# Cross-attention on one core: the first two blocks of x in halves of 256 columns, on ScalarE's queue

## What is computed

```
memory_proj = einsum('bme,de->bmd', memory, W_mem)
scores = einsum('bnd,bmd->bnm', x, memory_proj) / sqrt(512)
attn = softmax(scores)
memory_context = einsum('bnm,bmd->bnd', attn, memory_proj)
gate = sigmoid(einsum('bnf,df->bnd', concat([x, memory_context]), W_gate) + b_gate)
fused = x + gate * memory_context
out = fused * rsqrt(mean(fused**2) + 1e-6) * norm_w
```

## Time and profile before

| | us |
|---|---|
| median of 3 runs | 124.92 |
| lowest, highest | 123.68, 125.67 |
| the profiled execution, whole | 122.92 |
| its span in the trace | 121.2 |
| PE busy | 112.8 (93%) |
| DVE busy | 76.1 (63%) |
| ACT busy | 55.1 (45%) |
| POOL busy | 19.0 (16%) |

### The profile page before, as it was taken

One profiled execution on the slowest core, in us unless ns is written; L12 is line 12 of the kernel. 1 busy time (PEld: TensorE's weight loads), 2 busy tenths in 40 slices (PEclk: granted clock), 3 DMA queues, 4 the chain that ended last, 5 costly groups with the idle time before them and its releaser, 6 DMA issues.

```text
span 121.2 us, 1531 instructions
## 1 busy us (share of the span) xinstructions
PE 112.8 (93%) x529; PEld 92.8 (77%) x529; DVE 76.1 (63%) x115; ACT 55.1 (45%) x99; POOL 19.0 (16%) x25
## 2 busy tenths in 40 slices
PE   6899999999999999999999999999899999999900
PEld 6778788688888888888888888888588888888800
DVE  0398979977999700459982899947620032764791
ACT  4587575468967930942305365252500030423231
POOL 2000000000000499691000301010200000011040
PEclk9999999999999999999999999999999999999995
DMA  3999993236864690000455583847720000053204
GB/s 69 316 378 323 390 355 96 103 139 176 233 225 175 197 286 16 0 0 0 173 157 195 177 288 131 275 170 209 224 87 0 5 0 0 0 171 89 87 18 155
DMA packets 11095, 18.45 MB, mean 152 GB/s; under 512 B 1232, under 2 KB 4048, under 8 KB 11088
## 3 DMA queue, kind: packets, MB, share of 16 engines
q1 hardware_dynamic: 10656, 17.70, 43.9%
q10 hardware_dynamic: 432, 0.66, 1.9%
HBM read 14.16 MB, written 4.19 MB: 151 GB/s over the span
## 4 chain that ended last, share of the span: by engine, by line
PE 57%; DVE 14%; DMA 13%; issue 7%; ACT 3%; SPq 2%; POOL 1%; POOLq 1%; DVEq 0%; ACTq 0%
PE acc L758 18%; PE wide L708 12%; PE acc L683 8%; DMA ring<-passage 5%; DMA passage<-ring 5%; PE wide L736 5%; PE wide L786 4%; PE wide L774 4%; DVE neg_max L479 4%; PE wide L801 3%; DMA ring<-xT 3%; PE wide L722 3%; DVE ring L497 3%; DVE pT_lo L503 2%; SPq L277 2%
## 5 line engine op out<-in xcount | busy, mean ns | idle before, releaser
L322 POOL TENSOR_TENSOR rstd<-mean_sq,neg_half 128x1 f32<-128x1 f32 x8 | 5.4, 672 | 57.6 <-ACT squares L393 56.5
L520 DVE TENSOR_TENSOR wgT_lo<-acc,wgT_hi 128x512 fp32r<-128x512 f32 x4 | 2.6, 686 | 17.6 <-ACT wgT_hi L382 17.6
L708 PE MATMUL wide<-ctxT_hi,qT_lo 128*128 128x512 f32 x32 | 12.6, 393 | 0.0
L708 PE MATMUL wide<-ctxT_hi,qT_hi 128*128 128x512 f32 x32 | 12.6, 392 | 0.0
L357 ACT ACTIVATE probs<-wide,neg_max 128x1024 f32<-128x1024 f32 x8 | 8.9, 1115 | 8.0 <-DVE neg_max L479 8.0
L708 PE MATMUL wide<-ctxT_lo,qT_hi 128*128 128x512 f32 x32 | 12.5, 390 | 0.0
L386 ACT ACTIVATE gate<-gate 128x512 f32<-128x512 f32 x8 | 5.1, 632 | 15.1 <-DVE gate L530 15.1
L317 POOL TENSOR_TENSOR wgT_lo<-ring,wgT_hi 128x512 fp32r<-128x512 f32 x4 | 5.4, 1374 | 39.7 <-ACT wgT_hi L343 39.7
L479 DVE TENSOR_REDUCE neg_max<-wide 128x1 f32<-128x1024 f32 x8 | 9.8, 1222 | 2.2 <-PE wide L708 1.9
L758 PE MATMUL acc<-pT_lo,ctxN_hi 128*128 128x512 f32 x32 | 10.0, 393 | 0.5 <-DVE pT_lo L503 0.5
L758 PE MATMUL acc<-pT_hi,ctxN_lo 128*128 128x512 f32 x32 | 9.9, 390 | 0.0
(11 more groups left out here) (89 smaller groups left out, 244.8 us busy)
## 6 DMA issues: line engine op xcount, KB each, us to landing
ring<-ctxT SPq DMA_DIRECT2D x8, 256.0 KB, 4.1
ring<-w_gateT SPq DMA_DIRECT2D x8, 256.0 KB, 4.9
ring<-ctxN SPq DMA_DIRECT2D x8, 256.0 KB, 4.3
xr<-x_rows SPq DMA_DIRECT2D x8, 256.0 KB, 3.2
passage<-ring SPq DMA_DIRECT2D x4, 512.0 KB, 2.9
ring<-passage SPq DMA_DIRECT2D x16, 128.0 KB, 2.8
out<-res SPq DMA_DIRECT2D x7, 256.0 KB, 2.0
ring<-xT SPq DMA_DIRECT2D x6, 256.0 KB, 5.6
```

What stands on the lines that cost most here:

```text
L322: nc.gpsimd.tensor_tensor(rstd[:, col], mean_sq[:, col], neg_half[:], ALU.pow)\
L708: last = nc.tensor.matmul(wide[:, banks("scores", j), h], qT_s[left][:, c, rows], ctxT_s[right][:, c, cols], start=(c == 0 and (left, righ ...
```

## The change

The first two x blocks of batch 0 become four: x0 columns 0 to 255, x0 columns 256 to 511, x1 likewise. Each has its own place in the block list, its own ring slot (only half used) and its own splits. All four are issued by ACT. The block list has 40 entries instead of 38, so the hand-written numbers and `FIRST_ON_POOL` rise by two. On PE the 12 matmuls of 512 columns for k = 0 and 1 become 24 of 256.

```
-        def xT_block(b, k):
-            block(("xT", b, k), xT[b, :, k], xT_s, b, k)
+        def xT_block(b, k, cols=slice(0, N)):
+            block(("xT", b, k, cols.start), xT[b, :, k, cols], xT_s, b, k, cols)
...
+        X_HALVES = (slice(0, N // 2), slice(N // 2, N))
         wm_block(0, 0)
-        xT_block(0, 0)
+        for cols in X_HALVES:
+            xT_block(0, 0, cols)
         wm_block(1, 0)
-        xT_block(0, 1)
+        for cols in X_HALVES:
+            xT_block(0, 1, cols)
...
-        FIRST_ON_POOL = 28
-
-        BY_ACT = (index_of["xT", 0, 0], index_of["xT", 0, 1])
+        FIRST_ON_POOL = 30
+
+        BY_ACT = [index_of["xT", 0, k, cols.start] for k in range(2) for cols in X_HALVES]
...
-            split_hi(0, 1, 2, 3, 4, 5, 6, 7, 8)
+            split_hi(0, 1, 2, 3, 4, 5, 6, 7, 8, 9, 10)
...
-            split_lo(0, 1, 2, 3, 4, 5, 6, 7, 8)
+            split_lo(0, 1, 2, 3, 4, 5, 6, 7, 8, 9, 10)
...
-                    wm_i, xT_i = index_of["wm", c, 2 * k // KD], index_of["xT", b, k]
-                    for left, right in ((HI, HI), (LO, HI), (HI, LO)):
-                        if (left, right) == (HI, HI):
-                            wait_hi(pe, wm_i)
-                            wait_hi(pe, xT_i)
...
-                        last = nc.tensor.matmul(acc[:, c], wm_s[left][:, c, k], xT_s[right][:, b, k],
-                                                start=(k == 0 and (left, right) == (HI, HI)),
...
+                    wm_i = index_of["wm", c, 2 * k // KD]
+                    for cols in X_HALVES if b == 0 and k < 2 else (slice(0, N),):
+                        xT_i = index_of["xT", b, k, cols.start]
+                        for left, right in ((HI, HI), (LO, HI), (HI, LO)):
...
+                            last = nc.tensor.matmul(acc[:, c, cols], wm_s[left][:, c, k], xT_s[right][:, b, k, cols],
+                                                    start=(k == cols.start == 0 and (left, right) == (HI, HI)),
```

More of the change, by code:

```diff
@@ L394, in mean_square @@
                                      accum_out=mean_sq[:, j:j + 1]).then_inc(squared, 1)
-            split_hi(0, 1, 2, 3, 4, 5, 6, 7, 8)
+            split_hi(0, 1, 2, 3, 4, 5, 6, 7, 8, 9, 10)
             query_hi(0, 0)
-            split_hi(9, 10)
+            split_hi(11, 12)
             query_hi(0, 1)
-            split_hi(11, 12, 13)
+            split_hi(13, 14, 15)
             exponentials(0)
-            split_hi(14, 15)
+            split_hi(16, 17)
             exponentials(1)
-            split_hi(16)
+            split_hi(18)
             exponentials(2)
             turned_hi(0)
-            split_hi(17, 18)
+            split_hi(19, 20)
             turned_hi(1)
@@ L410, in _ @@
             query_hi(1, 0)
-            split_hi(19)
+            split_hi(21)
             query_hi(1, 1)
             turned_hi(2)
-            split_hi(20, 21)
+            split_hi(22, 23)
             weight_hi(0)
             turned_hi(3)
-            split_hi(22, 23)
+            split_hi(24, 25)
             weight_hi(1)
-            split_hi(*range(24, 34))
+            split_hi(*range(26, 36))
             attended_hi(0, 0)
             attended_hi(0, 1)
-            split_hi(*range(34, NB))
+            split_hi(*range(36, NB))
             exponentials(4)
@@ L582, in finish_last @@
                                         ALU.mult).then_inc(last_left, 1)
-            split_lo(0, 1, 2, 3, 4, 5, 6, 7, 8)
+            split_lo(0, 1, 2, 3, 4, 5, 6, 7, 8, 9, 10)
             query_lo(0, 0)
-            split_lo(9, 10)
+            split_lo(11, 12)
             query_lo(0, 1)
-            split_lo(11, 12)
+            split_lo(13, 14)
             row_max(0)
-            split_lo(13)
+            split_lo(15)
             row_max(1)
             normalize(0)
-            split_lo(14)
+            split_lo(16)
             row_max(2)
             normalize(1)
-            split_lo(15)
+            split_lo(17)
             normalize(2)
-            split_lo(16)
+            split_lo(18)
             turned_lo(0)
-            split_lo(17)
+            split_lo(19)
             row_max(3)
             turned_lo(1)
-            split_lo(18)
+            split_lo(20)
             normalize(3)
             query_lo(1, 0)
-            split_lo(19)
+            split_lo(21)
             query_lo(1, 1)
             turned_lo(2)
-            split_lo(20)
+            split_lo(22)
             weight_lo(0)
-            split_lo(21)
+            split_lo(23)
             turned_lo(3)
-            split_lo(22, 23)
+            split_lo(24, 25)
             weight_lo(1)
-            split_lo(24, 25, 26, 27)
+            split_lo(26, 27, 28, 29)
             attended_lo(0, 0)
@@ L673, in queries @@
                 for k in ks:
-                    wm_i, xT_i = index_of["wm", c, 2 * k // KD], index_of["xT", b, k]
-                    for left, right in ((HI, HI), (LO, HI), (HI, LO)):
-                        if (left, right) == (HI, HI):
-                            wait_hi(pe, wm_i)
-                            wait_hi(pe, xT_i)
[L679 to L682, removed]
-                        last = nc.tensor.matmul(acc[:, c], wm_s[left][:, c, k], xT_s[right][:, b, k],
-                                                start=(k == 0 and (left, right) == (HI, HI)),
-                                                stop=(k == KD - 1 and (left, right) == (HI, LO)))
+                    wm_i = index_of["wm", c, 2 * k // KD]
+                    for cols in X_HALVES if b == 0 and k < 2 else (slice(0, N),):
+                        xT_i = index_of["xT", b, k, cols.start]
+                        for left, right in ((HI, HI), (LO, HI), (HI, LO)):
+                            if (left, right) == (HI, HI):
+                                wait_hi(pe, wm_i)
+                                wait_hi(pe, xT_i)
+                            elif left == LO:
+                                wait_lo(pe, wm_i)
+                            else:
+                                wait_lo(pe, xT_i)
+                            last = nc.tensor.matmul(acc[:, c, cols], wm_s[left][:, c, k], xT_s[right][:, b, k, cols],
+                                                    start=(k == cols.start == 0 and (left, right) == (HI, HI)),
+                                                    stop=(k == KD - 1 and (left, right) == (HI, LO)))
                 if ks[-1] == KD - 1:
```

## The result

The changed kernel takes 128.1 us in the median of six executions (127.55 to 130.55), the kernel before 125.3 (six, 123.08 to 126.0): slower, by a ratio of 1.0346 with a 95% interval of 1.0231 to 1.0462. The profiled execution took 128.24 us, its span is 126.5. One thing has to be said for the ratio to be understood: three of the six executions of the kernel before (125.67 to 126.0 us) are left out of the comparison as disturbed, as are 18 of its 60 in all jobs together (125.06 to 128.44), so the ratio is that of 127.96 to 123.68 us, where the two medians above stand at 1.022.

A forecast was written before the change was run, and what follows sets the result against it. PE, busy for 93% of the span, was taken to bound the kernel; the first stage's terms summed to +0.3 us, passed on unchanged, taking the median from 124.92 to 125.2 us, range 123.9 to 126.5.

The forecast's parts named there:

- (c): PE's queries: 24 matmuls of 256 columns at 0.125 us replace 12 of 512, +0.27 us, covered by gaps.
- (a): ScalarE's queue: four issues instead of two delay the table load to 2.60; ACT's first split +0.1 us, at about 4.08.
- (b): First x half lands at about 4.0 instead of 4.56, so PE begins at about 4.95, 0.4 us earlier.
- The cover: PE's first gaps, 0.4 us together, plus 0.4 from (b), were to hide the narrow matmuls' +0.27 us.
- (d): DMA: x rows of 1 KB instead of 2 KB add 0.2 us; fourth x block lands at 8.28 instead of 8.08.
- (e): Arrival order: fourth half lands at 6.6 to 7.3, last x split at 8.4 to 8.5; PE's matmul +0.3 us.
- (f): Ring: two more slots delay the first two ctxT loads to about 4.9 and 5.4; priced at nothing.
- Rival 2: DMA: 1 KB rows as dear as 2 KB ones, fourth x block 1.36 us later; 126.3 us, chance 0.15.
- Rival 3: PE's clock falls to 1.2 GHz at the start, costing about 3 to 5 us; 128 to 130, chance 0.02.

The follow-up runs named there:

- TensorE's part alone: The kernel before with only the 12 products of k = 0 and 1 as 24 of 256 columns, loads and splits whole: 127.32 us, ratio 1.0244.
- the 22 of the same size at the wait: The changed kernel with 22 small matmuls on zeros in front of the attended product of batch 1: 127.0 us, ratio 1.0207.
- without the instruction count: The changed kernel with 4 warm-up matmuls fewer, 18 tiny ones, and 8 small matmuls before the attended product: 125.26 us, ratio 1.0112.
- the shorter warm-up: The changed kernel with 23 warm-up matmuls of 256 columns instead of 35 of 128, 24 TensorE instructions fewer: 125.53 us, ratio 1.0137.

## Why the prediction was wrong

- **Only the first stage was summed** ("if the first stage ends d later or earlier, all that follows should shift by about d"). This rule is the step that failed. It carried the start's 1.2 us faithfully to 59.2, and then there were 4.1 us more, from a transfer that no term of mine named and from the fall of the clock behind it. Part (c) priced 24 more instructions by their time on TensorE; they also move the moment at which TensorE's code is loaded. I had the row in front of me, "q8 instruction: 4" in the page of before, and passed it over as 0.2%.
- **(a)** Table load at 2.67, ACT's first split at 4.08: right.
- **(b)** First query at 4.93: right (4.95). But the other half had its price: it landed 1.0 us later than the whole block had.
- **(c)** 0.12 per narrow matmul against 0.125: right, though the working doesn't come out as it is told: half of 0.227 is 0.114, and 384 columns stand 0.008 above their share, not 0.02. TensorE's part alone moved the scores by 0.14. The cover was in part misread: 5.36 to 5.81 isn't a gap but the lower clock, at which products of 512 columns stand 0.43 apart.
- **(d), (e)** Here both the size and the place were off. The four halves landed at 3.45, 5.59, 7.19 and 7.72, the last of them beyond my 6.6 to 7.3. Behind it ACT took 1.5 us to the last x split, as computed (1.6), which gave 9.20 instead of 8.4 to 8.5. But PE hardly waited there: the weight load in front of the 30th query matmul (10.75) stood idle for 0.21 us, and the last block added 0.08. The path that (e) left out is the short one, from x0's second half and x1's halves straight to PE; up to k = 2 it cost 1.11, the narrow matmuls' own price included. I had taken the last block for the one that rules, because in the kernel before it arrives just in time.
- The Trainium skill's table ("DMA: Bandwidth & Descriptors", section "Bandwidth"), from which I had estimated 1.2 us for two more transfers, happens to give the 1.19 us by which the scores were late. That is luck as far as these runs go: the last x block, behind all the transfers, landed 0.6 us later, and x1's halves 1.3 and 1.8 us later than x1 had. No run shows a fixed price per transfer.
- **(f)** The ring: ctxT was waited for by nobody in the changed kernel, although its first two loads were issued at 5.03 and 5.46. Right.
- **Rival 2** came near the delay at the start, 1.4 us against 1.19, but not by its mechanism: it needs the last x block to land 1.36 us later, and that landed 0.6 later. A row price of 85 ns is refuted by this.
- **Rival 3**, the clock: it fell, at 91 us and not at 5. I had looked for it where the change is. And my reading that the clock stood at 1.00 at the start was wrong: the 35 matmuls of the warm-up stand 0.107 us apart, where the 22 of the same size at the wait stand 0.056 apart. They ran at 1.2 GHz, in both kernels, though the earlier trace rows and the page show full clock there.
- **The range.** It held the start's error and the spread of before, and would have held the changed kernel without the instruction count (125.26, or 125.53 with the shorter warm-up). It had no room for what came later, and neither had the 0.04 for slower.

## What to carry to other kernels

A change that adds instructions to an engine moves every later fetch of its code; if transfers on the critical path lie under it, a few dozen instructions more or less can cost more than the edit gains, and a control with as many idle instructions tells the two apart. Look in the trace for the transfers of kind "instruction" and for what is in flight beside them before calling a distant loss a shift. Splitting a load to have its first half early bought nothing here: TensorE began 0.43 us earlier and then waited for the second half, which landed 1.0 us later than the whole block had. Ask for the last part's landing, not for the first's.

## What the runs showed of the hardware

- A transfer of 16 KB of instructions (0.9 to 1.1 us where it met them) beside the rows of a critical transfer lengthens that one by 1 to 2 us: the second tile's send from 3.5 to 4.6, 4.75 and 4.97, the first tile's fetch from 2.84 to 3.82, 4.78 and 4.81. The third of them moved from 55.3 us behind the start of the scores to 53.2 with 24 more TensorE instructions and to 49.3 with 52 more, while nothing else had changed in that order.
- TensorE's clock fell to 1.2 GHz after idling of 2.57, 2.84, 2.11, 1.59, 1.14 and 1.07 us in front of the attended product, and not after 0.90, 0.91, 1.03, 1.17, 1.21 and 1.30: around 1.1 to 1.3 us of idling both happened. A fall cost 1.3 to 1.6 us here.
- The 35 matmuls of the warm-up stand 0.107 us apart, at 1.2 GHz. The clock came up between 3.9 and 6.8 us in most profiles, but at 9.0, 9.9 and 13.4 in three, and in one it fell again from 8.1 to 11.5. Before the first query TensorE had idled 2.0 us in the one of 9.0, 2.57 in the one of 13.4 and 2.14 in the one where it fell again, but not at all in the one of 9.9.
- Transfers of 128 KB on ScalarE's queue beside a busy SyncE queue landed 0.5 to 2.1 us apart (3.45, 5.59, 7.19, 7.72), two of 256 KB 1.3 us apart (4.56, 5.90). Why that is stays open.
